# Attention and ternary feed-forward on one core: column sums on the other side of the array, two warm-up jobs, masks copied first, and a new written-out order

## The reference

```python
xn = _layernorm(x, axis=-1)
x = x + attention(xn, Wq, Wk, Wv, Wo) + ffn(xn, W_fc, ln_w, ln_b, W_proj)

# attention: 16 heads of 16, each query sees itself and the 63 tokens before it
scores = jnp.einsum('bhld,bhlwd->bhlw', q, k_win) * scale      # w: window of 64
attn = jax.nn.softmax(jnp.where(invalid, -jnp.inf, scores), axis=-1)
ctx = jnp.einsum('bhlw,bhlwd->bhld', attn, v_win)              # then @ Wo

# ffn: 256 -> 1024 -> 256, both weights rounded to -1, 0, 1
h = gelu(jnp.einsum('btd,hd->bth', x, absmean(W_fc)), approximate=False)
h = layernorm(h, ln_w, ln_b)
out = jnp.einsum('bth,dh->btd', h, absmean(W_proj))
```

## Time and profile before

| | |
|---|---|
| median of 3 runs | 398.92 us (398.86 to 400.45) |
| profiled execution, own time | 397.85 us |
| span of its instructions | 396.0 us |
| busy: PE, DVE, ACT, POOL | 373.7, 321.2, 287.6, 231.4 us |
| mean granted TensorE clock | 0.996 |
| moved by DMA | 29.22 MB |

### The profile page before, as it was taken

One profiled execution on the slowest core, in us unless ns is written; L12 is line 12 of the kernel. 1 busy time (PEld: TensorE's weight loads), 2 busy tenths in 40 slices (PEclk: granted clock), 3 DMA queues, 4 the chain that ended last, 5 costly groups with the idle time before them and its releaser, 6 DMA issues.

```text
span 396.0 us, 13503 instructions
## 1 busy us (share of the span) xinstructions
PE 373.7 (94%) x5820; PEld 268.1 (68%) x5820; DVE 321.2 (81%) x645; ACT 287.6 (73%) x329; POOL 231.4 (58%) x186
## 2 busy tenths in 40 slices
PE   0698898999999999999999999999999999999995
PEld 0346565776577776876677775876677775778873
DVE  3898878699869998699959898599968898998555
ACT  2764249887986698767986698777977598768871
POOL 7901023866586548655576548655576647769871
PEclk9999989999999999999999999999999999999999
DMA  7459009600940267021910258021930256002002
GB/s 272 153 78 123 2 10 181 87 19 5 165 51 18 48 125 134 2 65 33 198 30 18 48 116 142 4 63 33 190 38 17 52 97 109 2 17 66 30 29 82
DMA packets 30685, 29.22 MB, mean 74 GB/s; under 512 B 5665, under 2 KB 29281, under 8 KB 30625
## 3 DMA queue, kind: packets, MB, share of 16 engines
q1 hardware_dynamic: 30624, 28.35, 36.6%
HBM read 7.35 MB, written 4.19 MB: 29 GB/s over the span
## 4 chain that ended last, share of the span: by engine, by line
PE 85%; DMA 4%; DVE 4%; ACT 3%; SPq 2%; issue 1%; POOL 1%; POOLq 1%; ACTq 0%
PE small L1600 15%; PE big L1539 13%; PE big L1513 11%; PE small L1611 10%; PE big L1590 7%; PE big L1578 5%; PE big L1553 5%; PE big L1525 5%; PE small L1627 5%; PE big L1583 4%; PE big L1559 4%; DMA mask_k<-mask_k 2%; SPq L374 2%; DMA gel<-in_w_fc 2%; PE small L1617 2%; PE big L1501 2%
## 5 line engine op out<-in xcount | busy, mean ns | idle before, releaser
L578 POOL TENSOR_TENSOR p_parts<-probs,p_parts 128x1024 f16<-128x1024 f32 x64 | 136.2, 2132 | 112.8 <-ACT p_parts L762 112.8
L761 ACT ACTIVATE probs<-big,exp_scale 128x1024 f32<-128x1024 f32 x64 | 71.4, 1116 | 22.9 <-PE big L1583 20.7
L1016 DVE TENSOR_REDUCE negmax<-big 128x8 f32<-128x1024 f32 x64 | 77.6, 1222 | 7.1 <-PE big L1559 5.7
L762 ACT ACTIVATE p_parts<-big,exp_scale 128x1024 f16<-128x1024 f32 x64 | 71.3, 1115 | 0.0
L1600 PE MATMUL small<-proj_t,g_hi 128*128 128x256 f16 x256 | 57.7, 273 | 0.0
L1600 PE MATMUL small<-proj_t,g_lo 128*128 128x256 f16 x256 | 57.5, 273 | 0.0
L776 ACT ACTIVATE g_hi<-big,lnw_s 128x512 f16<-128x512 f32 x64 | 39.8, 690 | 17.2 <-PE big L1590 17.2
L1539 PE MATMUL big<-fc_t,xt_hi 128*128 128x512 f16 x128 | 48.5, 379 | 1.0 <-DVE g_lo L1010 1.0
L1539 PE MATMUL big<-fc_t,xt_lo 128*128 128x512 f16 x128 | 48.6, 379 | 0.0
L1010 DVE SCALAR_TENSOR_TENSOR g_lo<-big,lnw_s,g_hi 128x512 f16<-128x512 f32 x64 | 46.5, 746 | 2.2 <-ACT g_hi L776 1.8
L749 ACT ACTIVATE gel<-big 128x1024 f32<-128x1024 f32 x32 | 32.7, 1025 | 12.6 <-PE big L1539 12.2
(11 more groups left out here) (130 smaller groups left out, 812.2 us busy)
## 6 DMA issues: line engine op xcount, KB each, us to landing
q_stack<-qk_split SPq DMA_DIRECT2D x48, 128.0 KB, 4.0
k_stack<-qk_split SPq DMA_DIRECT2D x48, 128.0 KB, 5.3
x_in<-in_x SPq DMA_DIRECT2D x8, 512.0 KB, 5.5
out<-y_bufs SPq DMA_DIRECT2D x32, 128.0 KB, 2.4
v_odd<-v_even SPq DMA_DIRECT2D x16, 132.0 KB, 2.5
v_odd<-v_even SPq DMA_DIRECT2D x16, 99.0 KB, 2.2
gel<-in_w_fc SPq DMA_DIRECT2D x1, 1024.0 KB, 6.7
y_bufs<-in_w_proj SPq DMA_DIRECT2D x1, 1024.0 KB, 8.8
```

Of the source, the lines that this page charges most:

```text
L578: g.tensor_tensor(p_lo[:, (b * NJ + j) % PB], probs[:, (b * NJ + j) % PB], p_hi[:, (b * NJ + j) % PB], ALU.subtract).then_inc(*sig(p_lo_re ...
L761: s.activation(probs[:, (b * NJ + j) % PB].rearrange("p i (u q) -> p u i q", u=2), st, ACT.Exp, scale=exp_scale[:, 0:1]).then_inc(*sig(exp ...
L762: s.activation(p_hi[:, (b * NJ + j) % PB].rearrange("p i (u q) -> p u i q", u=2), st, ACT.Exp, scale=exp_scale[:, 0:1]).then_inc(*sig(p_hi ...
L1016: v.tensor_reduce(negmax[:, :, j], slot[b, "sa", j][:].rearrange("p a (u k) -> p (a u) k", k=P), AX.X, ALU.max, negate=True).then_inc(*sig ...
```

## The change

`crow` multiplied one column of ln_w or ln_b (three bf16 parts) as the stationary operand with 256 columns of `proj_t`, 48 times, and had the sums in one row. Now `proj_t` is the stationary operand, in 16 blocks of 128x128, and the moving one has 6 columns (three parts of both vectors), so that the sums come out one to a partition. DVE adds the three parts and multiplies the identity with each column (`mean_term` is borrowed for it), and `csum` multiplies ones with these diagonal matrices.

A new job `warm` of four matmuls of 512 columns, which reads `onehot` and writes to a buffer that nobody reads, stands after `sums` 0 and after `spread` 1. `copy_masks` moves ahead of the first stacks on SP. In `ORDER` and in all engines' lists many neighbours trade places: `fc` 3 of batch 0 before the first `sa`, `sums` 1 after the first `fc`, `pv` 3 before `sa` 7, `st` 2 directly after `st` 1, `shift_values(b, 1)` behind the stacks of batch b + 1, `load_x` ahead of `shift_values(b, 0)`, in the last batch `v` before `gt` 1.

```diff
-        crow = sb("crow", [1, 2 * D], fp32)
+        ccol = sb("ccol", [P, KD, 2], fp32)
...
-        FIRST = [(0, "wmax", 0), (0, "spread", 0), (0, "sums", 0), (0, "wmax", 1), (0, "xt", 0), (0, "spread", 1),
+        FIRST = [(0, "wmax", 0), (0, "spread", 0), (0, "sums", 0), (0, "warm", 0), (0, "xt", 0), (0, "wmax", 1),
...
-            jobs = [j for j in ORDER if (j[1] in IN_BIG) == is_big]
+            jobs = [j for j in ORDER if (j[1] in IN_BIG) == is_big and j[1] != "warm"]
...
             load_x(1)
+            copy_masks()
             load_stack(0, 0, 0)
             load_stack(0, 0, 1)
             load_stack(0, 1, 0)
             load_stack(0, 1, 1)
-            copy_masks()
+            load_maxima(0)
             shift_values(0, 0)
-            load_maxima(0)
+            load_x(2)
             load_stack(1, 0, 0)
-            load_x(2)
-            shift_values(0, 1)
             load_stack(1, 0, 1)
             load_stack(1, 1, 0)
             load_stack(1, 1, 1)
+            shift_values(0, 1)
+            load_x(3)
             shift_values(1, 0)
...
             def copy_row():
                 dve.wait_ge(*at(0, crow_done, 1))
-                v.tensor_copy(crow[:], slot[0, "crow", 0][0:1, :]).then_inc(*sig(crow_copied))
+                link_pre(v.tensor_reduce(ccol[:], slot[0, "crow", 0][:, 0:6 * KD].rearrange("p (h a c) -> p h c a", h=KD, c=2),
+                                         AX.X, ALU.add))
+
+                for c in range(2):
+                    for h in range(KD):
+                        last = v.tensor_scalar(mean_term[:, c, h * P:(h + 1) * P], ident[:], ccol[:, h, c:c + 1], None, ALU.mult)
+                last.then_inc(*sig(crow_copied))
...
             def job(b, kind, n):
-                ps = slot[b, kind, n]
-                wait_slot(pe, (b, kind, n))
-                if kind == "xt":
+                if kind != "warm":
+                    ps = slot[b, kind, n]
+                    wait_slot(pe, (b, kind, n))
+                if kind == "warm":
+
+                    if n == 0:
+                        pe.wait_ge(onehot_ready, 1)
+                    flat = onehot[:].rearrange("p i q -> p (i q)")
+                    for i in range(WARM[n]):
+                        mm(big[2][:, 1], flat[:, 0:P], flat, start=True, stop=True)
+                elif kind == "xt":
...
-                    for c in range(2):
-                        i = 0
+                    for h in range(KD):
                         for k in range(NH):
-                            for part in range(3):
-                                last = mm(ps[0:1, c * D:(c + 1) * D], lnv_parts[:, part, c, k:k + 1], proj_t[:, k],
-                                          start=(i == 0), stop=(i == 3 * NH - 1))
-                                i += 1
+                            last = mm(ps[:, h * 6:(h + 1) * 6], proj_t[:, k, h * P:(h + 1) * P],
+                                      lnv_parts[:, :, :, k], start=(k == 0), stop=(k == NH - 1))
                     last.then_inc(*sig(crow_done))
                 elif kind == "csum":
                     pe.wait_ge(*at(b, crow_copied, 1))
-                    mm(ps[:], ones[0:1, :], crow[:], start=True, stop=True).then_inc(*sig(csum_done))
+                    for c in range(2):
+                        last = mm(ps[:, c * D:(c + 1) * D], ones[:], mean_term[:, c], start=True, stop=True)
+                    last.then_inc(*sig(csum_done))
```

More of the change, by code:

```diff
@@ L844, in _ @@
             gelu(2, 1)
+            gelu(2, 2)
             context_upper(0, 0)
-            gelu(2, 2)
             gelu(2, 3)
@@ L886, in _ @@
                 gelu_upper(p + 3, 1)
+                qk_upper(p + 4, 0)
+                exp(p + 2, 6)
+                gelu_upper(p + 3, 2)
+                gelu_upper(p + 3, 3)
+                exp(p + 2, 7)
+                qk_upper(p + 4, 1)
+                gelu_upper(p + 3, 4)
+                gelu_upper(p + 3, 5)
+                gelu_upper(p + 3, 6)
+                gelu_upper(p + 3, 7)
+                exp(p + 3, 0)
+                gelu(p + 4, 0)
+                context_upper(p + 2, 0)
+                gelu(p + 4, 1)
+                gelu(p + 4, 2)
+                gelu(p + 4, 3)
+                exp(p + 3, 1)
+                v_upper(p + 4)
+                exp(p + 3, 2)
+                exp(p + 3, 3)
+                normalize(p + 5)
+                exp(p + 3, 4)
+            xt_upper(6)
+            exp(4, 5)
+            context_upper(3, 1)
+            gelu_upper(5, 0)
+            gelu_upper(5, 1)
             qk_upper(6, 0)
@@ L1220, in _ @@
             maximum(1, 6)
+            maximum(1, 7)
             add_projection(0, 3)
-            maximum(1, 7)
+            scale_context(0, 3)
             gelu_lower(1, 0)
-            scale_context(0, 3)
             gelu_lower(1, 1)
@@ L1261, in _ @@
             maximum(2, 6)
+            maximum(2, 7)
+            scale_context(1, 3)
             context_lower(0, 1)
-            maximum(2, 7)
             gelu_lower(2, 0)
-            scale_context(1, 3)
             gelu_lower(2, 1)
@@ L1305, in _ @@
             maximum(3, 6)
+            maximum(3, 7)
+            scale_context(2, 3)
             context_lower(1, 1)
-            maximum(3, 7)
             gelu_lower(3, 0)
-            scale_context(2, 3)
             gelu_lower(3, 1)
@@ L1394, in _ @@
             maximum(6, 6)
+            maximum(6, 7)
+            scale_context(5, 3)
             context_lower(4, 1)
-            maximum(6, 7)
             gelu_lower(6, 0)
-            scale_context(5, 3)
             gelu_lower(6, 1)
```

241 lines of the change are left out of this document (114 added, 127 removed), and 86 rows, old and new, of tables (FIRST, LAST, PERIOD).

## The result

The changed kernel takes 400.93 us in the median of 20 runs (398.30 to 404.35), the kernel before 397.83 in 20 runs beside them (396.09 to 400.45): ratio 1.0067, 95% interval 1.0047 to 1.0087. On another chip, later, the same changed kernel gave 1.0030 (0.9999 to 1.0061). So it is slower by 0.67% beside the first 20 runs; in the second measurement, 0.30%, the interval just reaches no change. The forecast was 0.25% faster. The range on record, 395.6 to 400.8, held 10 of the 20 runs, and their median lies 0.13 us above it.

What follows compares the result with a forecast made beforehand. It took PE as the bound, busy 94% of the span and never waiting from about 62 to 382 us. Terms -1.2 - 0.8 + 0.5 + 0.0 + 0.5 = -1.0 us gave a median of 397.9, range 395.6 to 400.8.

Steps and rivals of the forecast that it cites:

- q done: Head, PE: batch 0's q matmuls end at 21.7 us, 0.35 before the old time; bounds 20.4 and 22.4.
- last k_stack landed: Head, DMA: the q and k stack copies, 1.05 us apart, have landed at 37.8 us.
- first score job: Head, PE: starts at 37.8 us at full clock or 39.0 at half, after stacks and fc(0,3).
- first maximum: Head, DVE: at 39.4 us, before 40.64; term -1.2 us, bounds -2.1 and -0.3.
- period: Middle: 44.8 us each, no buffer release waits; term 0.0 us (-0.5 to +0.8).
- the head: Start up to batch 0's second score job: forecast -2.0 us, from terms -1.2 and -0.8.
- The stretch at half clock from 49.0: Batch 0's maxima, PE: 0.3 of 1.5 us counted as saved, with 0.49 of DVE's wait -0.8.
- The copies of v: First value product, SP's queue: v copies behind batch 1's stacks make a wait of +0.5 us (0 to 1.2).
- The end: Last batch: scale_context(6,6) releases (6, pv, 7) later, st(7,3) moves the third exp; +0.5 us (-0.5 to +1.1).
- Rival (b): Between v and column sums: idle PE loses its clock and stays slow; +2.5, 401.4 us; chance 0.10.
- (a): Head gives all: clock up before q, kept while PE idles; -2.7, 396.2 us; chance 0.32.
- (c): Middle: v's buffer from gelu(·,3) lacks room, five periods lose some 0.6 each; +2.0, 400.9 us; chance 0.08.

Runs made afterwards that it cites:

- e15: The changed kernel itself, measured again on the chip of e13 and e14; median 399.59 us, ratio 1.0030 to the kernel before.
- e5: The changed kernel with gelu(0,2) put back on ACT ahead of v's upper part and normalize(1); median 397.41 us, ratio 0.9988.
- e2: The changed kernel with the second part of batch 0's v copies moved ahead of x(2) and batch 1's stacks; 398.90 us, ratio 1.0037.
- e6: The changed kernel with SP's order of the kernel before for batch 0's copies of v; median 398.61 us, ratio 1.0044.
- e13: The changed kernel with the edits of e5 and e6 together; median 397.50 us, ratio 0.9991.
- e7: The kernel before in every order, no warm jobs, late masks, only column sums and constant products in new form; 400.43 us, ratio 1.0069.
- e4: The changed kernel with 14 filler matmuls between v of batch 0 and the column sums; median 398.30 us, ratio 1.0007.
- e12: The changed kernel with the edits of e5 and e4, and the old order from batch 7's last fc job on; 395.78 us, ratio 0.9933.
- e14: e12 with SP's order of the kernel before for batch 0's copies of v; median 396.13 us, ratio 0.9959.

## Why the prediction was wrong

| step on record | said | measured |
|---|---|---|
| transposes of x behind the first warm job | 13.4 | 13.44 |
| q done | 21.7 | 22.08 (20.32 in e15) |
| `copy_row` | 1.0 | 1.06 (37.98 to 39.04) |
| PE idle before the sums, ended by proj_t | 3.3 | 3.12, proj_t |
| column sums | 0.4 | 0.42 |
| last k_stack landed | 37.8 | 38.78 (37.15 in e15) |
| DVE ready for its first maximum | 38.1 | 39.04 |
| first score job | 37.8 or 39.0 | **40.36** |
| first maximum | 39.4 | **41.48** |
| pv(0,0) waits for v_odd | +0.5 (0 to 1.2) | **2.10** |
| period | 44.8 | 44.76 |
| end | +0.5 (-0.5 to +1.1) | +1.15 |

**The step that failed** is "The first score job starts at 37.8 or 39.0". It asked what data the job needs (stacks, masks, fc(0,3) off PE) and not what it writes to: its PSUM buffer is released by gelu(0,2), which the change had put behind normalize(1). The prediction went through every buffer's release for one period and not for the head, the only part where orders differ in more than a place or two. e5 shows it: with that line back the first score job follows the stacks and starts 1.47 us earlier. So 1.5 us of the head's gains were taken by a wait I had not listed.

With the repair the head is 2.12 us shorter than before, where -2.0 was on record, but that the sum agrees is luck. The first maximum of e5 stands at 40.01, a gain of 0.63 where I had 1.2: the last stack landed at 38.80, not at 37.8, since q got the full clock at 20.28 in this execution (37.0 to 37.6 in those where it came by 16.1 and stayed). From there to (0, st, 1) it takes 28.69 us, in the changed kernel too, against 30.18: a gain of 1.49 where I had 0.8. The stretch at half clock from 49.0, of which I counted 0.3 of 1.5 us, did not come back there.

**The copies of v**: the mechanism was right, the term mis-sized, +0.5 against +3.1 in this execution, the largest miss of its trace. pv(0,0) starts 7.76 us behind st(0,1), and 5.58 where nothing holds it up (e2, e6): 2.2 us are the wait. Batch 1's score jobs then take 42.54 us to those of batch 2, with the half clock of 78.5 in them, against 41.4 in e5 and e6: 1.1 us more. That I counted landings by 1.05 us a copy and took one number for them is the error: the last one landed 9.09 us after its issue here and 7.72 in e5. In the median the term may be as small as I said (e13).

**The end**: the term was right in sign, 0.65 too small, and its main releaser was another: scale_context(6,6) holds up (6, pv, 7) for 0.11 us, g_lo holds up st(7,2) for 0.58. Counted from (7, sa, 0), (7, proj, 0) comes 0.46 us later than before, where I had 0.1; the other 0.7 are made behind it, where I had 0.4.

**Rival (b)**, idle PE loses its clock, had 0.10. Its mechanism is there (e7, e4), and by the mean clock of the executions, 0.990 against 0.9967, more of it came than that chance allowed for. It did not come as it was priced: in the changed kernel's trace the clock was back at 44.35, before xt(1), and the score jobs at half clock start 0.85 us apart where DVE needs 1.15 for each maximum, so that stretch was covered. What it does cost comes when a stretch falls later, on transposes and qk, as in e6, where (0, gt, 0) came 10.94 us behind the first score job instead of 9.60. The Trainium skill, TensorE: Matmul & The Clock Gate, section Why this matters for your kernels, ties the half clock to idle gaps between bursts; e7 agrees (7.13 us idle), and so does e15, whose clock fell at 76.88 behind 1.96 us. In the kernel before it fell at 48.99 with no gap over 0.5 us in the 8 us ahead, so here gaps are not the whole of it. **(a)** and **(c)** did not come: no period waits.

Why one execution of an order gets one such stretch and the next three stays open, and so does why the copies of v land late in some.

**A better version.** e12, the changed kernel with three repairs, is faster than both: 0.9933 (0.9907 to 0.9958). e14, with the copies of v put back too, is at 0.9959 (0.9925 to 0.9993) and has the shortest span, 392.5.

## What to carry to other kernels

When an order is moved, go through two lists at every place where an engine waits: what the job reads, and who must finish with the buffer that it writes, above all at the head, where the steady order's room does not exist. Work that is "covered" by a wait may be what keeps TensorE's clock up: taking 5 us of it away cost 0.7% here (e7). 14 matmuls of no use, put into the changed kernel's gap, raised its mean clock from 0.990 to 0.996 and brought it back to 1.0007 (e4). Where single executions lie 6 us apart, a profile tells where a wait is and only a median tells what it is worth.
